# Attention and FFN in one kernel on one core: the FFN products from scaled fp16 pairs instead of fp32r pairs, with the weight scaling on GpSimd

## What is computed

```python
xn = layernorm(x)                                  # (2, 1024, 512)
s  = attention(xn, Wq, Wk, Wv, Wo)                 # 16 heads, causal
up_gate, up_lin = xn @ W1.T, xn @ W3.T             # (2, 1024, 2048) each
hidden = fwht(silu(up_gate) * up_lin)
out = x + s * silu(hidden @ W2.T)
```

## Time and profile before

| | |
|---|---|
| median of 3 runs | 972.14 us (972.06 to 972.33) |
| profiled execution | 972.55 us, span 970.8 us |
| TensorE busy | 959.4 us (99% of the span) |
| VectorE busy | 707.1 us (73%) |
| ScalarE busy | 565.7 us (58%) |
| GpSimd busy | 357.2 us (37%) |
| heads, batch 0 and batch 1 | about 88 to 370 us and 569 to 850 us |

### The profile page before, as it was taken

The page is one execution under the profiler, slowest core; times in us unless marked ns, Lnnn a source line. Parts: engine busy times, 40 slices in busy tenths (PEclk is TensorE's granted clock), DMA queues, the critical chain, the costliest instruction groups (busy, mean ns, idle before and its releaser), DMA issues. The chain is left out here.

```text
span 970.8 us, 18488 instructions
## 1 busy us (share of the span) xinstructions
PE 959.4 (99%) x6392; PEld 797.7 (82%) x6392; DVE 707.1 (73%) x1441; ACT 565.7 (58%) x1172; POOL 357.2 (37%) x587
## 2 busy tenths in 40 slices
PE   8999999999999999999999999999999999999997
PEld 7888888888888887888888888888888888878886
DVE  7777888888888887755554578888888888833343
ACT  4324777777777786623334166777777777832221
POOL 1896764656656442000001024453443543500000
PEclk9999999999999999999999999999999999999999
DMA  9793235232232405951145523233223232181111
GB/s 285 259 271 110 77 89 142 78 88 56 77 89 56 121 23 201 345 203 44 45 174 204 174 55 88 57 78 89 55 78 88 56 78 56 45 342 49 43 44 44
DMA packets 55757, 110.58 MB, mean 114 GB/s; under 512 B 5360, under 2 KB 22384, under 8 KB 55152
## 3 DMA queue, kind: packets, MB, share of 16 engines
q1 hardware_dynamic: 55664, 109.40, 37.1%
HBM read 75.56 MB, written 33.55 MB: 112 GB/s over the span
## 5 line engine op out<-in xcount | busy, mean ns | idle before, releaser
L1024 DVE TENSOR_TENSOR p_lo<-stage,p_hi 128x512 f16<-128x512 f32 (+2 forms) x288 | 188.3, 654 | 58.4 <-ACT p_hi L743 58.0
L1337 PE MATMUL f<-xt_hi,w_hi 128*128 128x512 f32 x512 | 202.0, 394 | 0.0
L1337 PE MATMUL f<-xt_hi,w_lo 128*128 128x512 f32 x512 | 201.8, 394 | 0.0
L1337 PE MATMUL f<-xt_lo,w_hi 128*128 128x512 f32 x512 | 201.5, 394 | 0.0
L733 ACT ACTIVATE stage<-s 128x512 f32<-128x512 f32 (+2 forms) x288 | 150.8, 524 | 82.9 <-PE s L1298 81.1
L743 ACT ACTIVATE p_hi<-stage 128x512 f16<-128x512 f32 (+2 forms) x288 | 158.8, 551 | 24.9 <-POOL stage L595 20.2
L1298 PE MATMUL s<-qk_st 98*128 98x512 f32 (+2 forms) x384 | 141.4, 369 | 0.0
L1011 DVE CUSTOM_DVE_ANT_0 m<-m,causal 128x1024 f32<-128x1024 f32 (+3 forms) x128 | 131.0, 1023 | 2.7 <-PE m L1282 2.7
L602 POOL TENSOR_TENSOR w_lo<-w,w_hi 128x256 fp32r<-128x256 f32 x128 | 118.3, 953 | 28.5 <-ACT w_hi L764 27.2
L595 POOL TENSOR_SCALAR_AFFINE_SELECT stage<-stage 128x128 f32<-128x128 f32 x192 | 57.4, 306 | 179.0 <-ACT stage L733 178.2
L1337 PEld LDWEIGHTS f<-xt_lo,w_hi 128*128 128x128 f32 x512 | 96.6, 189 | 18.2
(11 more groups left out here) (179 smaller groups left out, 1831.3 us busy)
## 6 DMA issues: line engine op xcount, KB each, us to landing
qk_st<-qk_parts SPq DMA_DIRECT2D x96, 256.0 KB, 4.3
w<-w1w SPq DMA_DIRECT2D x32, 512.0 KB, 3.6
qk_parts<-qk_hi SPq DMA_DIRECT2D x32, 256.0 KB, 3.2
qk_parts<-qk_lo SPq DMA_DIRECT2D x32, 256.0 KB, 4.3
wht_in<-w SPq DMA_DIRECT2D x4, 1024.0 KB, 10.9
w_butterflied<-wht_in SPq DMA_DIRECT2D x4, 1024.0 KB, 5.9
w_transformed<-g_hi SPq DMA_DIRECT2D x8, 512.0 KB, 3.2
w_transformed<-g_lo SPq DMA_DIRECT2D x8, 512.0 KB, 4.7
```

Source lines behind the costliest of these rows:

```text
L1024: dve.tensor_tensor(p_lo[s][:], expd[q % NE][:, 0:end - need], p_hi[s][:], ALU.subtract).then_inc(p_lo_done, 1)
L1337: mm = pe.matmul(F[m][:, 0, :], w, v, start=k == 0, stop=k == GMM - 1)
```

## The change

**New operands.** The input of the FFN gets fp16 parts of its own: `x16_hi` and `x16_lo` are the transposed xn times 2048 (`X_TOP`), rounded on ScalarE and completed on VectorE, 8 tiles in each batch, in `project`. The fp32r parts stay for Q, K and V. The tiles of W1/W3 are multiplied by a power of two and split into fp16 parts.

**Scales.** The power of two comes from the sum of squares of a tile: ScalarE squares it with an accumulator (`w13_squares`), TensorE adds over the partitions with a matmul against ones (`sum_of_squares`, six times), VectorE makes four factors from the exponent bits in five small instructions (`scale_of_w13`, six times). That is done in batch 0 only, on a separate load of every tile but the first (`scan_w13`, 15 loads of 512 KB): three of them in `project`, the other 12 in heads 0 to 11, one in step 5 of a head. tanh and `hide` take the factors back out.

**Where the weights are scaled.** `w13_high` scales while it copies. For the lo part GpSimd scales the tile in place (`tensor_scalar`, two of 128x512 a head) ahead of the four subtractions; the first tile of a batch is scaled by ScalarE. `w13_high` of a batch's first tile moves from group 8 to the second group of V.

**Not changed.** The number, shape and order of the FFN matmuls in a step, and the order of score, maxima and context matmuls. Buffers are laid out anew in SBUF; `qk_hi`, `qk_lo`, `xt_hi`, `xt_lo` keep their waits, but the transposes of xn and `bound_of_v` now wait for the x16 tiles that are read from their PSUM banks.

```diff
+X16_AFTER = {2: (0,), 3: (1,), 4: (2, 3), 7: (6, 7), 8: (4,), 9: (5,)}
+SCAN_AFTER = {10: (1,), 13: (2, 3)}
+SQUARES_AFTER = {8: (0,), 13: (1,)}
+SQUARES_OF_V = {4: (2,), 5: (3,)}
+SCAN_FIRST, SCAN_GROUP = 4, 3
...
# SyncE
+            def scan_w13(t):
+                if t > SCAN_FIRST:
+                    sp.wait_ge(w13_sum, t)
...
+                sp.dma_start(scan_tile(t), w1w3[t]).then_inc(scan_in[t % 3], 16)
...
                         load_stack(sp, n + 2)
+                        if b == 0 and j + SCAN_FIRST < NH:
+                            scan_w13(j + SCAN_FIRST)
                         load_w13(n + 2)
# GpSimd
-                pool.tensor_tensor(w13_lo[n % 2][at], w13[at], w13_hi[n % 2][at].bitcast(F32), ALU.subtract
+                if piece % 2 == 0 and n % NH > 0:
+                    pool.tensor_scalar(w13[:, piece // 2, :], w13[:, piece // 2, :], w13_scale[:, n % NH:n % NH + 1],
+                                       None, ALU.mult).then_inc(w13_scaled, 1)
+                pool.wait_ge(w13_scaled, 2 * n + piece // 2 + 1)
+                pool.tensor_tensor(w13_lo[n % 2][at], w13[at], w13_hi[n % 2][at], ALU.subtract
# ScalarE
+            def x16(b, t):
+                act.wait_ge(xt_lo_done, b * NT + t + 1)
+                act.activation(x16_hi[:, :, t * P:(t + 1) * P], xt_bank(t).rearrange("p (k c) -> p k c", k=KT),
+                               ACT.Copy, scale=X_TOP).then_inc(x16_hi_done, 1)
...
+            def w13_squares(n):
...
+                act.activation(scan_tile(n) if n else w13_hi[0][:], scan_tile(n), ACT.Square,
+                               accum_out=w13_ssq[:, n:n + 1]).then_inc(w13_sum, 1)
...
+                    if b == 0 and s == SQUARES_AT and j + SCAN_FIRST < NH:
+                        w13_squares(j + SCAN_FIRST)
                     if s == W13_AT and j + 1 < NH:
                         w13_high(n0 + j + 1)
# VectorE
+            def x16(b, t):
+                dve.wait_ge(x16_hi_done, x16_no(b, t))
...
+                dve.scalar_tensor_tensor(x16_lo[at], xt_bank(t).rearrange("p (k c) -> p k c", k=KT), X_TOP,
+                                         x16_hi[at], ALU.mult, ALU.subtract).then_inc(x16_lo_done, 1)
...
-                dve.tensor_tensor(hidden_part(n, c), hidden_part(n, c), F[1][:], ALU.mult
+                dve.scalar_tensor_tensor(hidden_part(n, c), hidden_part(n, c), w13_unscale[:, n % NH:n % NH + 1],
+                                         F[1][:], ALU.mult, ALU.mult).then_inc(hidden_done, 1)
# TensorE
                 if t >= 4:
-                    pe.wait_ge(xt_lo_done, b * NT + t - 3)
+                    pe.wait_ge(x16_lo_done, x16_no(b, t - 4))
...
                 pe.wait_ge(ones_ready, 2)
                 pe.wait_ge(xt_lo_done, NT)
+                pe.wait_ge(x16_lo_done, x16_no(0, 6))
...
+                pe.matmul(w13_sum_bank(n), ones_r[:].bitcast(F32), w13_ssq[:, tiles_of(n)], start=True, stop=True
+                          ).then_inc(w13_sum_ps, 1)
...
-                    v = (xt_hi, xt_lo, xt_hi)[p][:, kt, c * W:(c + 1) * W]
+                    v = (x16_hi, x16_lo, x16_hi)[p][:, kt, c * W:(c + 1) * W]
```

More of the change, by code:

```diff
@@ L129, in build @@
         w13 = sb("w13", [P, 2, D], F32)
-        stage = [sb(f"stage{i}", [P, D], F32) for i in range(3)]
+        stages = sb("stages", [P, 3, D], F32)
+        stage = [stages[:, i, :] for i in range(3)]
         stats = sb("stats", [P, NT, 6], F32)
@@ L254, in split_no @@
             return b * NQ + i
[L256 removed]
+        raw = [*stage, w13[:, 0, :], w13[:, 1, :]]
         def weights_loaded(b, i):
@@ L295, in xt_bank, with w13_sum_bank, scan_tile, tiles_of @@
             return (SB[0][:, 0, :], SB[1][:, 0, :], M[:, 0, :], M[:, 1, :])[t % 4]
+        def w13_sum_bank(n):
+            return X[:, 0, W - len(scan_groups[n]):W]
+        scan_groups = [range(1), range(1, SCAN_FIRST)] + [range(t, t + SCAN_GROUP) for t in range(SCAN_FIRST, NH, SCAN_GROUP)]
+        SUM_PLAN = {scan_groups[n][-1] - SCAN_FIRST: n for n in range(1, len(scan_groups))}
+        def scan_tile(t):
+            if t < SCAN_FIRST:
+                return (w13[:], stages[:, 0:2, :], wv_raw[:, 0:2, :], wv_raw[:, 2:4, :])[t]
+            return scan[:]
+        def tiles_of(n):
+            return slice(scan_groups[n][0], scan_groups[n][-1] + 1)
+        def scale_steps(t):
+            return 5 * next(n + 1 for n, tiles in enumerate(scan_groups) if t in tiles)
+        def x16_no(b, t):
+            return b * NT + X16_ORDER.index(t) + 1
         def score_cols(c, k):
@@ L423, in project @@
                         step(slab)
+                    if b == 0:
+                        for t in SCAN_AFTER.get(g, ()):
+                            scan_w13(t)
                     if g == KT:
@@ L714, in project @@
                             split_wv(b, kt)
-                    if g == 2 * KT:
-                        w13_high(b * NH)
+                    for t in X16_AFTER.get(g, ()):
+                        x16(b, t)
+                    if b == 0:
+                        for t in SQUARES_AFTER.get(g, ()):
+                            w13_squares(t)
                 if b == 0:
@@ L724, in project, with scale_first @@
                                    ACT.Copy).then_inc(proj_hi_done, 1)
+                    if t == 1:
+                        scale_first(b * NH)
+                        w13_high(b * NH)
+                    if b == 0:
+                        for tile in SQUARES_OF_V.get(t, ()):
+                            w13_squares(tile)
                     if t == MT_BEFORE - 1:
                         maxima_hi(b * NH)
+            def scale_first(n):
+                act.wait_ge(w13_in, (n + 1) * 16)
+                act.wait_ge(w13_scale_step, scale_steps(0))
+                for m in range(2):
+                    act.activation(w13[:, m, :], w13[:, m, :], ACT.Copy, scale=w13_scale[:, 0:1]).then_inc(w13_scaled, 1)
             def exp(q):
```

125 lines of the change are left out of this document (100 added, 25 removed).

## The result

The changed kernel takes **1008.3 us** (median of 4 runs, 1005.3 to 1017.2) against 972.2 of the kernel before beside it: ratio 1.038, 95% interval 1.035 to 1.040. It is slower by 36 us where 12 us less were forecast, and outside the range. Its profiled execution has a span of 1006.9 us at a granted clock of 0.995.

The account below looks back on a forecast made before the run. TensorE, 99% busy, was taken as the bound, so time moves with matmul spacing. The terms, -23.8 + 3.5 + 2.3 + 1.5 + 4.2 = -12.3 us on 972.55, gave 960.2, as a median 960.0 us; range 951 to 969.

Parts of the forecast that it names:

- Term 1: FFN matmuls on TensorE: fp16 brings starts from 231.5 to 216 ns apart, 1536 times; -23.8 us, between 0 and -28.
- term 2: Heads, TensorE: switching between fp32r and fp16 matmuls costs 10 ns at each of 352 entries; +3.5 us.
- Term 3: x16 tiles in `project`: hidden in batch 1, delaying group 8 and bound_of_v in batch 0; +2.3 us, between 0 and 4.
- Term 4: Six sums over partitions, each a small fp32 matmul on TensorE taken at 0.25 us; +1.5 us.
- Term 5: Batch 0's heads: ScalarE's square delays m_hi, m_lo and their DMAs; scores stall 0.35 us in 12 heads; +4.2 us.
- rival D: Batch 0's heads stall 0.9 us each: DMAs land later or ScalarE's delay reaches full VectorE; 966.6 us, chance 0.15.
- Term 6: GpSimd's two weight scalings a head, 0.86 us each, hidden with 0.6 us to spare; 0 us.
- Rival C: GpSimd becomes the bound: scaling takes 1.41 us, tile 0.5 us late in 30 heads, +15 us; 970.6 us, chance 0.12.

## Why the prediction was wrong

**Term 1 (spacing) was right.** 217 ns from start to start against 216 predicted; the 131 ns of the Trainium skill ("TensorE: Matmul & The Clock Gate", Back-to-back issue gap) did not appear here either. With **term 2** (type changes) it makes a head of 17.41 us, against 17.3 to 17.4 predicted; over 32 heads that is 19 us less than 18.00, where the two terms have 20.3.

**Term 3 (x16) was about right:** in batch 0's `project` group 8 starts 1.0 us later than before and `bound_of_v` 2.5 us later, against 2.3 predicted. Its rows, TensorE, against the earlier trace rows:

```profile
38.30 0.47 PE L1306 MATMUL f<-xt_hi,w_hi 128*128 128x512 f32 x1 [0.97 <-issue]
42.63 1.16 PE L1411 MATMUL m<-w_lo,ones_r 128*128 128x512 f32 x4 [1.36 <-DVE x_lo L1062]
```

What these three say is 972.1 - 23.8 + 3.5 + 2.3 = 954, 18 us less than before. The kernel without scans, without scaling and with the waiting butterfly measures 957.4, 15.7 less than the kernel before beside it (973.1).

**Term 4 (sums)** was small and too high: from the start of a sum to the next matmul's TensorE takes 0.14 us, 0.8 in all against 1.5.

**Term 5 (squares) came near for eleven heads by another path than its own, and missed the twelfth.** In the kernel with ScalarE's scaling and the waiting butterfly, eleven heads with a square are 0.47 us longer on average than in the one without scans (196.3 against 191.1 us; batch 1's heads are equally long in both, 17.34 and 17.33). Predicted was 0.35; the numbers there give 0.9 + 0.4 - 1.0 = 0.3, and a slack of 0.4 to 2.3 instead of 0.3 to 2.2. But scores that wait for the maxima's DMA, the predicted path, cost TensorE 0.3 us in one of the eleven. What its weight loads wait for in batch 0's heads is mostly VectorE, in waits that the kernel without scans doesn't have, and the heads differ, from 17.50 (three of them) to 18.46 us. So the nearness is luck in part; that ScalarE's delay reaches VectorE is what rival D named.

```profile
PEld xs L1439 <- DVE m_lo L1154: 3.0, 11, 0.3
PEld m L1439 <- DVE mx L1148: 2.8, 10, 0.5
PEld s L1455 <- DMA qk_st<-m_lo: 1.1, 2, 0.6
```

Head 4 is 6.5 us longer: the scan's DMA stands in SyncE's queue behind the 1 MB load of a slab. "Only its issue stands in SyncE's queue" was the sentence that failed: it counted the queue the scan is ahead of, not the one it is behind. SyncE, then ScalarE, changed kernel:

```profile
165.69 3.28 SPq L443 DMA_DIRECT2D wht_in<-w  x1
169.01 3.49 SPq L377 DMA_DIRECT2D qk_st<-qk_parts  x3
172.54 0.42 SPq L497 DMA_DIRECT2D scan<-w1w  x1
```

```profile
180.74 1.06 ACT L855 ACTIVATE scan<-scan 128x1024 f32<-128x1024 f32 x1 [5.00 <-DMA scan<-w1w]
```

**Term 6 (GpSimd's scaling, costed at nothing) is the step that turned the sign.** The mechanism, the place and even the threshold of 1.15 us stood in the text; the duration was wrong. I took 0.86 us by scaling up a small mask, and called 1.41, the two-input butterfly, the upper bound, since two inputs must be slower than one. Measured: 1.55 at least, 1.85 on average, 2.52 at most. A bound from another instruction was no bound. In the head shown above the two scalings took 4.08 us instead of the 1.72 of the sum; the four low parts, taken over at 3.80, took only 2.81 with fp16 as their output. Together 7.04 us against 5.72, 1.3 more where 0.6 were to spare: that is the late tile, 0.7 us. Without the shorter low parts, which no term had, it would have been a microsecond worse. Rival C was this case with half its size: it had 15 us for the late tile, and only named the load of the tile and `store_maxima` queued behind it, without a price. They cost as much again (0.86 beside 0.78 us a head). Had the second half been priced at the first's rate, C would have stood at 986, on the other side of zero. "The cover is gone above 1.15 us" was also a threshold that deserved more than 0.12: of the two rows it was taken between, the mask's and the butterfly's, one lay on either side of it.

**What no term had** is that VectorE and GpSimd hold each other up, which goes with the second scaling's 2.52 us beside two p_lo, and which took 6.4 us of the gain in batch 0's heads even without any scaling (963.7 to 957.4).

So the 36 us are: -16 from TensorE's side (957.4 against 973.1; it holds term 3's stalls too), +6 from butterflies that now meet p_lo, +13 from scans and +31 from scaling, in this order of adding. Unrounded they add to 35, since the kernel before was 0.8 us apart in the two comparisons. In another order the parts differ, as the kernel without scans shows.

## What to carry to other kernels

Before work is put on an idle engine, see what is queued behind it there and on the DMA queues that wait for its last piece: a late result costs once for its reader and once for everything behind it. A duration taken from another instruction of the same engine is no bound, even where that one does more; when the threshold lies near it, try the other engines too, here ScalarE, at 1.14 us a head and no time lost. And when a stretch gets shorter, here by 3%, instructions of two engines that just missed each other can begin to meet: if only some heads show the gain, compare the lengths of the same instruction in both.

## What the runs showed of the hardware

- **VectorE's subtraction of two SBUF operands and a GpSimd butterfly, which has two inputs, exclude each other, first come first served.** In batch 0's heads p_lo of 128x256 took 1.55 us behind a butterfly that had begun 0.01 us earlier (0.42 alone), and a wait that kept it ahead made it short and the kernel 6.4 us faster. With the multiply by a second tensor it looks alike: p_lo of 128x512 took up to 1.55 us beside it, 0.69 alone.
- **With the multiply by a pointer operand it is different.** One p_lo that came 0.02 us behind such a scaling kept its 0.70 us, and the scaling took 2.06; ten that came 0.2 us behind took 1.02; all but one of those that came 0.75 us or more behind kept their 0.69, although both ran at once. In the head shown above the first p_lo here began ahead of the scaling of 752.01 and took 1.18, the second began inside it and took 0.68, and the scaling took 2.52. Why is open.

```profile
751.39 1.18 DVE L1164 TENSOR_TENSOR p_lo<-stages,p_hi 128x512 f16<-128x512 f32 x1
752.50 0.68 DVE L1164 TENSOR_TENSOR p_lo<-stages,p_hi 128x512 f16<-128x512 f32 x1
```

- VectorE's maxima and its gate, which read PSUM, keep their length beside GpSimd (the gate 0.68 us inside a scaling and without one): this maximum of the changed kernel lies inside the scaling of 749.08.

```profile
749.17 0.82 DVE L1151 CUSTOM_DVE_ANT_0 m<-m,causal 128x640 f32<-128x640 f32 x1
```

  The Trainium skill, "GPSIMD Engine Reference" (1), says that GpSimd shares its SBUF interfaces with VectorE, with contention for VectorE's instructions with two SBUF inputs; by that the trace agrees, 1.55 against 0.42 us. For butterflies these rows show that whole instructions wait; for the low parts, whose partner grew by less than their length, it is not settled.
- **On GpSimd a multiply of 128x512 by a pointer operand took 1.56 us, and by a second tensor 1.04,** both in place in fp32. The Trainium skill, "GPSIMD Engine Reference" (3.1), gives 769 ns for 512 elements as its best case; the measured 1.56 is twice that and decides. Whether the pointer operand is the reason was not tried apart.
- A pointer operand costs ScalarE 0.08 us on the copy of a tile (1.139 against 1.058 us), and with ScalarE's scaling batch 1's heads stay at 17.41 us.
